# Two-layer cross attention in float32: layer 0's softmax weights are normalised in place and split by ScalarE and GpSimd, and the order of the work is written anew

## The chip, the cores and the metric

The kernel runs on one core of a Trainium2 chip. The metric is the device time of one execution, in microseconds. In the profile PE is TensorE (PEld its weight loads), DVE is VectorE, ACT is ScalarE, POOL is GpSimd, and SP only issues DMAs here. L12 is line 12 of the kernel's file.

## The reference

For each of 8 batches, x is [512, 256] and ctx is [1601, 128], all float32:

```python
# layer 0: softmax over axis 1, which is the 512 rows of x, for each of the 1601 columns
q = x @ Wq0 + bq0; k = ctx @ Wk0 + bk0; v = ctx @ Wv0 + bv0
w = softmax(q @ k.T * 256**-0.5, axis=rows_of_x)
x = layernorm(w @ v + x, eps=1e-6) * gamma + beta
# layer 1: softmax over the 1601 keys
Q = x @ Wq1 + bq1; K = ctx @ Wk1 + bk1; V = ctx @ Wv1 + bv1
out = x + (softmax(Q @ K.T * 256**-0.5, axis=keys) @ V) @ Wo + bo
```

## The kernel before, in words

The projections are folded: with A = Wq Wk^T the scores are (x A + b) ctx^T, so neither k nor v is ever made, and the weights act on ctx itself (128 columns) before one product with Wv. ctx is cut into 13 tiles of 128 rows (`MT` = 13, the last has 65), x into 4 row tiles of 128 (`TB` = 4).

Almost every large product keeps float32's accuracy by `split3`: an operand is held as a high part (rounded to the `fp32r` type) and a low part (exact minus high), and three matmuls go into one PSUM bank: w_lo times m_hi, w_hi times m_lo, w_hi times m_hi (L407 to L409, whoever calls them). ScalarE makes the high parts, VectorE or GpSimd the low ones.

Layer 0 for tile i (steps are functions of one batch and a tile number):

- `scores0` (PE): scores of 128 ctx rows against all 512 rows of x, in one of two banks of `ps_l0`.
- `max0` (DVE, L839): adds the bias row, scales, and finds the extreme of each row, out to `s0_sb`.
- `exp0` (ACT, L707): the exponential into `p0`, with its row sum; `recip0` (DVE, L846): 1/sum into `r0`.
- `p0_high` (ACT, L716): p0 times r0, rounded to `p0_hi`; `p0_low` (DVE, L851): p0 times r0 minus p0_hi, into `p0_lo`.
- `weigh0` (PE): p0_hi and p0_lo against ctx_hi and ctx_lo, summed over the 13 tiles in `ps_acc0`.
- `sum_weights` (POOL, L1034, L1037, L1039): adds p0_lo and then p0_hi to `wsum`, two additions a tile (one for the first).

`p0`, `p0_hi` and `p0_lo` have 5 places each (`ring0`: tile 12 has its own, the others take turns in four). Then `sum_rows0` (PE), `bias_x0` (DVE, L873), `weighed0` (ACT) and `at0_low` (DVE, L820), `predict` (PE), `residual0` (L883), `moments0`, `rsqrt_var` (POOL, L1058), `normalised` (L904), `turn_y` (PE, L483), `y_turned` (ACT, L729), `project_q1` (PE, L489), `q1_high` (ACT, L733), `q1_low` (DVE, L918).

Layer 1 for row tile t: `scores1` makes its 1601 scores in four chunks, one to a bank (402, 402, 402, 396 columns); `rowmax1` (DVE, L926) takes the maximum of each chunk, `bias1_of` (DVE, L934, L937) joins the four and adds the row's bias; `exp1` (ACT, L746) takes three banks and then the fourth. Then for each of the 13 ctx tiles `turn_p1` (PE transposes, L513), `p1_turned` (ACT, L754), `p1_low` (DVE, L858), `weigh1` (PE); at the end `project_out` (L527), `finish` (DVE, L953), and `residual1` on POOL (L1048, L1052) for the residual.

The order of the work is written out by hand. Four tables (`TENSOR_ORDER`, `SCALAR_ORDER`, `VECTOR_ORDER`, `GPSIMD_ORDER`) hold, for one body, each engine's steps; every engine runs its own in order, and semaphores hold them together. A body works on three batches at once: "c" is the newest (its first layer-0 tiles), "a" the one whose layer 0 it ends, "b" the one whose layer 1 it does:

```python
pre[0]()
body(None, None, batch(0, 0), AHEAD)
pre[1]()
body(batch(0, 0), None, batch(0, 1))
with eng.Fori(0, PAIRS) as pair:          # PAIRS = 3
    body(batch(pair, 1), batch(pair, 0), batch(pair, 2))
    body(batch(pair, 2), batch(pair, 1), batch(pair, 3))
body(batch(PAIRS, 1), batch(PAIRS, 0), None)
body(None, batch(PAIRS, 1), None)
```

So the pipeline fills in two bodies, six full bodies follow, then one without a "c", and one with a "b" alone. A full body begins on DVE with `q1_low`, whose eight starts in the trace (96.33, 159.77, 226.33, 291.98, 357.68, 424.67, 491.70 and 546.52 us) are taken as the edges of the bodies. The loop's semaphore waits are against registers. ctx is loaded by SP into one buffer `ctx_sb`, x by ACT's queue into two.

## Time and profile before

| what | value |
|---|---|
| median of 3 runs | 582.12 us (580.67 to 584.35) |
| span of the profiled execution | 583.1 us |
| its own time | the page gives the span alone; it lies within the runs' range |
| DVE busy | 493.2 us, 85% of the span |
| PE busy | 488.3 us, 84% |
| POOL busy | 368.2 us, 63% |
| ACT busy | 334.3 us, 57% |
| DMA | 17.25 MB, 30 GB/s on average |

Shares of the whole span mix the filling and the emptying of the pipeline with its steady part; what paces a body is read from windows laid on the bodies. A matmul's end in the profile is modelled, so a matmul's cost is read from start to start. Several engines' instructions overlap their neighbours a little (an instruction's write-back runs beside the next one), so sums of durations lie above busy time. The granted TensorE clock stands as PEclk in the windows, as a share of 2.4 GHz.

### The profile page before, as it was taken

Reading aid. Unit: us, or ns where it says so; the run is one execution under the profiler, and the core shown is the slowest. Engines: PE = TensorE matmul, PEld = TensorE weight load, DVE = VectorE, ACT = ScalarE, POOL = GpSimd, SP = SyncE. Lnnn points to the kernel's source line nnn. Section 1 sums busy time; section 2 is a strip of 40 time slices with the busy share of each in tenths; the row PEclk is TensorE's granted clock in tenths of the full one; section 3 lists DMA queues with packets and bytes.
Section 4 is the critical chain, followed back from the end, with each engine's and each line's share of the span. In section 5 each row is a group of like instructions: output and inputs, shape, how many; then the busy total and the mean of one; then the engine's idle time right before and its main releaser. Section 6 shows DMA issues by size and latency. Waiting matters only on the chain.

```text
span 583.1 us, 8934 instructions
## 1 busy us (share of the span) xinstructions
PE 488.3 (84%) x2426; PEld 397.4 (68%) x2426; DVE 493.2 (85%) x1088; ACT 334.3 (57%) x694; POOL 368.2 (63%) x319
## 2 busy tenths in 40 slices
PE   8679477898789987898889987898978986799777
PEld 8466355786578865786567865686767865677665
DVE  2577689889997988889998999889997999778864
ACT  3546634685457843785566843785546834573362
POOL 0377968757595848767695848767586758753400
...
DMA packets 23900, 17.25 MB, mean 30 GB/s; under 512 B 1055, under 2 KB 23854, under 8 KB 23854
## 3 DMA queue, kind: packets, MB, share of 16 engines
...
## 4 chain that ended last, share of the span: by engine, by line
DVE 40%; PE 36%; issue 15%; POOL 4%; ACT 4%; DVEq 1%; ACTq 0%; POOLq 0%
DVE p_lo L851 6%; PE ps_s L407 6%; DVE p1T_lo L858 5%; PE ps_s L409 4%; PE ps_s L408 4%; DVE max L926 4%; PE ps_l L407 4%; PE ps_s L513 4%; PE ps_l L409 4%; PE ps_l L408 4%; DVE xr L912 3%; DVE xr L873 3%; DVE bias L937 3%; DVE s_sb L839 3%; DVE xhat L904 2%
## 5 line engine op out<-in xcount | busy, mean ns | idle before, releaser
L1037 POOL TENSOR_TENSOR wsum<-wsum,p_lo 128x512 f32<-128x512 f32 x96 | 131.7, 1372 | 107.0 <-DVE p_lo L851 103.7
L1039 POOL TENSOR_TENSOR wsum<-wsum,p_hi 128x512 f32<-128x512 f32 x96 | 128.2, 1336 | 7.5
L707 ACT ACTIVATE p<-s_sb,min 128x512 f32<-128x512 f32 (+1 forms) x104 | 75.0, 722 | 70.2 <-DVE min L839 70.2
L851 DVE SCALAR_TENSOR_TENSOR p_lo<-p,r,p_hi 128x512 fp32r<-128x512 f32 (+1 forms) x104 | 103.6, 1008 | 2.0 <-ACT p_hi L716 2.0
L839 DVE CUSTOM_DVE_ANT_0 s_sb<-ps_l,cb 128x512 f32<-128x512 f32 (+1 forms) x104 | 70.4, 682 | 17.4 <-PE ps_l L409 13.6
L716 ACT ACTIVATE p_hi<-p,r 128x512 fp32r<-128x512 f32 (+1 forms) x104 | 74.8, 726 | 15.3 <-DVE r L846 10.4
L746 ACT ACTIVATE p<-ps_s,bias 128x1206 f32<-128x1206 f32 (+1 forms) x60 | 55.3, 925 | 47.5 <-DVE bias L937 47.4
L926 DVE TENSOR_REDUCE max<-ps_s 128x1 f32<-128x402 f32 x120 | 65.3, 570 | 19.0 <-PE ps_s L409 18.7
L407 PE MATMUL ps_s<-ctxT_hi,qw_lo 128*128 128x402 f32 x120 | 47.7, 398 | 35.9 <-DVE qw_lo L918 23.0
L858 DVE TENSOR_TENSOR p1T_lo<-ps_s,p1T_hi 128x512 fp32r<-128x512 f32 (+1 forms) x104 | 68.3, 679 | 8.9 <-ACT p1T_hi L754 8.9
L754 ACT CAST p1T_hi<-ps_s 128x512 fp32r<-128x512 f32 (+1 forms) x104 | 58.5, 586 | 22.3 <-PE ps_s L513 17.9
L513 PE MATMUL ps_s<-ident,p 128*128 128x128 f32 (+1 forms) x416 | 60.4, 280 | 4.1 <-ACT p L746 4.1
L513 PEld LDWEIGHTS ps_s<-ident,p 128*128 128x128 f32 (+1 forms) x416 | 52.0, 145 | 14.8 <-ACT p L746 4.8
L407 PEld LDWEIGHTS ps_s<-ctxT_hi,qw_lo 128*128 128x128 f32 x120 | 24.6, 205 | 46.1 <-DVE qw_lo L918 26.8
L407 PE MATMUL ps_l<-p_hi,ctx_lo 128*128 128x512 f32 (+1 forms) x104 | 48.7, 468 | 3.7 <-POOL ctx_lo L1025 3.7
L407 PE MATMUL ps_s<-p1T_hi,ctx_lo 128*128 128x512 f32 (+1 forms) x104 | 46.2, 444 | 0.0
L407 PE MATMUL ps_l<-qw_hi,ctxT_lo 128*128 128x512 f32 (+1 forms) x104 | 44.1, 424 | 0.6 <-DVE min L839 0.6
L408 PE MATMUL ps_s<-ctxT_lo,qw_hi 128*128 128x402 f32 x120 | 44.4, 370 | 0.0
L409 PE MATMUL ps_s<-ctxT_hi,qw_hi 128*128 128x402 f32 x120 | 44.4, 370 | 0.0
L408 PE MATMUL ps_l<-p_lo,ctx_hi 128*128 128x512 f32 (+1 forms) x104 | 42.6, 410 | 0.0
L409 PE MATMUL ps_l<-p_hi,ctx_hi 128*128 128x512 f32 (+1 forms) x104 | 42.6, 410 | 0.0
L409 PE MATMUL ps_l<-qw_hi,ctxT_hi 128*128 128x512 f32 (+1 forms) x104 | 42.0, 404 | 0.0
...
## 6 DMA issues: line engine op xcount, KB each, us to landing
...
```

The lines of the kernel that those rows point to most:

```text
L407: nc.tensor.matmul(ps, w_lo, m_hi, start=start, stop=False)
L408: nc.tensor.matmul(ps, w_hi, m_lo, start=False, stop=False)
L409: return nc.tensor.matmul(ps, w_hi, m_hi, start=False, stop=stop)
L513: mm = nc.tensor.transpose(ps_turn[i % 3][0:m, t * P:(t + 1) * P], p1[:, t, i * P:i * P + m], ident[:])
L707: nc.scalar.activation(p0[0:m, ring0(i), :], s0_sb[0:m, (a.par + i) % 2, :], ACT.Exp, bias=min0[0:m, i:i + 1], scale=-1.0, accum_out=sum0[ ...
L716: nc.scalar.activation(p0_hi[0:m, ring0(i), :], p0[0:m, ring0(i), :], ACT.Copy, scale=r0[0:m, i:i + 1]).then_inc(p0_hi_done, 1)
L839: nc.vector.tensor_tensor_reduce(out=s0_sb[0:m, (a.par + i) % 2, :], in0=ps_s0[0:m, (a.par + i) % 2, :], in1=cb[a.par][0:m, :], scale=-SCA ...
L851: nc.vector.scalar_tensor_tensor(p0_lo[0:m, ring0(i), :], p0[0:m, ring0(i), :], r0[0:m, i:i + 1], p0_hi[0:m, ring0(i), :].bitcast(F32), AL ...
L858: nc.vector.tensor_tensor(p1T_lo[0:m, i % RING, :], ps_turn[i % 3][0:m, :], p1T_hi[0:m, i % RING, :].bitcast(F32), ALU.subtract).then_inc( ...
L926: nc.vector.tensor_reduce(max1[:, t, k:k + 1], s1_banks(b, t)[:, k, 0:min(hi, M) - lo], AX_X, ALU.max).then_inc(max1_done, 1)
L1037: nc.gpsimd.tensor_tensor(total, total, lo, ALU.add).then_inc(wsum_part, 1)
L1039: nc.gpsimd.tensor_tensor(total, total, hi, ALU.add).then_inc(wsum_done, 1)
```

## The change

- `norm0` is new (ACT): it multiplies `p0` by `r0` in place. `p0_high` becomes a plain cast of the normalised `p0` (ACT), and `p0_low` moves from DVE to POOL as one subtraction.
- `sum_weights` adds the normalised `p0` itself: one addition a tile, and tiles 0 and 1 in one instruction (12 in all instead of 25).
- `p0` keeps its 5 places; `p0_hi` and `p0_lo` have 3. `exp0` now waits until `weigh0` and `sum_weights` are done with the tile before it in its place, and `p0_high` and `p0_low` wait for `weigh0` three tiles back. `SPLIT` names the tiles that are split; it holds all 13, so the other branch of `weigh0` is not taken.
- `rowmax1` takes two banks at a time (2 x 402 columns, two instructions a row tile instead of four). For that the fourth chunk is shifted to begin at column 1199, so that it is 402 wide too; `exp1` skips what overlaps. `bias1_of` is a tensor_scalar instead of a scalar_tensor_tensor.
- `ctx_sb` has two buffers; its loads wait for the batch two before. x is loaded by SP instead of ACT's queue. Batch 1's ctx is loaded at the start.
- The loop over pairs is unrolled, so all waits are on constants.
- All four order tables are new. `project_q1` now stands last in PE's table and `q1_high` near the end of ACT's, and PE does two tiles of `scores0` and one of `weigh0` before the first `scores1`.

```diff
-    ("q1_low", "b", 0), ("max0", "a", 6), ("p0_low", "a", 5), ("rowmax1", "b", 0), ("rowmax1", "b", 1),
+    ("q1_low", "b", 0), ("max0", "a", 6), ("max0", "a", 7), ("rowmax1", "b", 0), ("rowmax1", "b", 1),
...
+    R0 = 4
+    RH = 3
+    SPLIT = tuple(range(MT))
...
+        back, last = (1, i) if i == MT - 1 else ((0, i - R0) if i >= R0 else (1, i + MT - 1 - R0))
+        return None if back and first(a) else (back, last)
...
+    def split_before(a, i):
+
+        j = SPLIT.index(i) - RH
+        if j >= 0:
+            return MT * a.n + SPLIT[j] + 1
+        return None if first(a) else MT * (a.n - 1) + SPLIT[j] + 1
+
+    def summed(n, i):
+
+        return (MT - 1) * n + max(i, 1)
...
-    chunks = [(c, min(MPAD, c + CHUNK)) for c in range(0, MPAD, CHUNK)]
+    chunks = [(c, c + CHUNK) for c in range(0, last_lo, CHUNK)] + [(M - CHUNK, M)]
+    skip = last_lo - (M - CHUNK)
...
-            with eng.Fori(0, PAIRS) as pair:
+            for pair in range(PAIRS):
...
-                if a and c:
+                if b and c:
+                    sp.wait_ge(xbias_done, c.n - 1)
+                    load_x(c)
                     for g in range(GROUPS):
                         load_ctx(c, g, after=True)
...
             def exp0(a, i):
                 act.wait_ge(s0_read, MT * a.n + i + 1)
-                if (n := before0(a, i)) is not None:
-                    act.wait_ge(p0_lo_done, n)
+                if (held := before0(a, i)) is not None:
+                    back, last = held
+                    act.wait_ge(pv0_ps, MT * (a.n - back) + last + 1)
+                    act.wait_ge(wsum_done, summed(a.n - back, last))
...
+            def norm0(a, i):
+                act.wait_ge(r0_done, MT * a.n + i + 1)
+                m = rows(i)
+                nc.scalar.activation(p0[0:m, ring0(i), :], p0[0:m, ring0(i), :], ACT.Copy, scale=r0[0:m, i:i + 1]
+                                     ).then_inc(norm0_done, 1)
+
             def p0_high(a, i):
-                act.wait_ge(r0_done, MT * a.n + i + 1)
-                if (n := before0(a, i)) is not None:
-                    act.wait_ge(pv0_ps, n)
-                    act.wait_ge(wsum_done, n)
+                act.wait_ge(norm0_done, MT * a.n + i + 1)
+                if (held := split_before(a, i)) is not None:
+                    act.wait_ge(pv0_ps, held)
                 m = rows(i)
-                nc.scalar.activation(p0_hi[0:m, ring0(i), :], p0[0:m, ring0(i), :], ACT.Copy, scale=r0[0:m, i:i + 1]
-                                     ).then_inc(p0_hi_done, 1)
+                nc.scalar.copy(p0_hi[0:m, split_place(i), :], p0[0:m, ring0(i), :]).then_inc(p0_hi_done, 1)
...
-            def p0_low(a, i):
-                dve.wait_ge(p0_hi_done, MT * a.n + i + 1)
-                m = rows(i)
-                nc.vector.scalar_tensor_tensor(p0_lo[0:m, ring0(i), :], p0[0:m, ring0(i), :], r0[0:m, i:i + 1],
-                                               p0_hi[0:m, ring0(i), :].bitcast(F32), ALU.mult, ALU.subtract
-                                               ).then_inc(p0_lo_done, 1)
...
-                nc.vector.tensor_reduce(max1[:, t, k:k + 1], s1_banks(b, t)[:, k, 0:min(hi, M) - lo], AX_X, ALU.max
+                nc.vector.tensor_reduce(max1[:, t, k:k + 1], s1_banks(b, t)[:, 2 * k:2 * k + 2, 0:CHUNK], AX_XY, ALU.max
                                         ).then_inc(max1_done, 1)
...
-                nc.vector.scalar_tensor_tensor(bias1[:, t:t + 1], neg_max1[:, t:t + 1], c1[:, t:t + 1], c1[:, t:t + 1],
-                                               ALU.subtract, ALU.add).then_inc(bias1_done, 1)
+                nc.vector.tensor_scalar(bias1[:, t:t + 1], neg_max1[:, t:t + 1], c1[:, t:t + 1], c1[:, t:t + 1],
+                                        ALU.subtract, ALU.add).then_inc(bias1_done, 1)
...
-                    pool.wait_ge(wsum_done, MT * a.n + i)
-                    nc.gpsimd.tensor_tensor(total, total, lo, ALU.add).then_inc(wsum_part, 1)
-                    pool.wait_ge(wsum_part, (MT - 1) * a.n + i)
-                    nc.gpsimd.tensor_tensor(total, total, hi, ALU.add).then_inc(wsum_done, 1)
+                    pool.wait_ge(wsum_done, summed(a.n, i - 1))
+                    nc.gpsimd.tensor_tensor(total, total, p0[0:m, ring0(i), :], ALU.add).then_inc(wsum_done, 1)
+
+            def p0_low(a, i):
+                pool.wait_ge(p0_hi_done, split_count(a.n, i))
+                if (held := split_before(a, i)) is not None:
+                    pool.wait_ge(pv0_ps, held)
+                m, h = rows(i), split_place(i)
+                nc.gpsimd.tensor_tensor(p0_lo[0:m, h, :], p0[0:m, ring0(i), :], p0_hi[0:m, h, :].bitcast(F32),
+                                        ALU.subtract).then_inc(p0_lo_done, 1)
```

What stands on the engines at three places. First DVE, where a full body begins (`qw_lo` is the low part of layer 1's query, `s_sb,min` the scores of layer 0, `max` the maxima of layer 1). Before:

```order
L918 SCALAR_TENSOR_TENSOR qw_lo<-ps_s,scaled,qw_hi 128x512
L318 ISA
L839 ISA s_sb,min<-ps_l,cb 128x512
L839 ISA min 128x1
L851 SCALAR_TENSOR_TENSOR p_lo<-p,r,p_hi 128x512
L925 ISA
L926 TENSOR_REDUCE max<-ps_s 128x1
```

The same place now:

```order
L944 SCALAR_TENSOR_TENSOR qw_lo<-ps_s,scaled,qw_hi 128x512
L872 ISA s_sb,min<-ps_l,cb 128x512
L872 ISA min 128x1
L872 ISA s_sb,min<-ps_l,cb 128x512
L872 ISA min 128x1
L951 TENSOR_REDUCE max<-ps_s 128x1 x2
L959 TENSOR_REDUCE neg_max<-max 128x1
L962 TENSOR_SCALAR bias<-neg_max,c 128x1
```

`p_lo` is gone from DVE, a second tile of layer 0's scores stands in its place, and two reductions do for four.

Second PE, at the turn from one body to the next: the last product of a body is `project_q1` (`xhT,a_gamma`), and the first product of layer 1's scores reads `qw_lo`. Before:

```order
L489 MATMUL ps_s<-xhT,a_gamma 128x512 x2
L407 MATMUL ps_l<-p_hi,ctx_lo 128x512
L408 MATMUL ps_l<-p_lo,ctx_hi 128x512
L409 MATMUL ps_l<-p_hi,ctx_hi 128x512
L407 MATMUL ps_s<-ctxT_hi,qw_lo 128x402
```

And now:

```order
L520 MATMUL ps_s<-xhT,a_gamma 128x512 x2
L432 MATMUL ps_l<-p_hi,ctx_lo 128x512
L433 MATMUL ps_l<-p_lo,ctx_hi 128x512
L434 MATMUL ps_l<-p_hi,ctx_hi 128x512
L432 MATMUL ps_l<-qw_hi,ctxT_lo 128x512
L433 MATMUL ps_l<-qw_lo,ctxT_hi 128x512
L434 MATMUL ps_l<-qw_hi,ctxT_hi 128x512
L432 MATMUL ps_l<-qw_hi,ctxT_lo 128x512
L433 MATMUL ps_l<-qw_lo,ctxT_hi 128x512
L434 MATMUL ps_l<-qw_hi,ctxT_hi 128x512
L432 MATMUL ps_s<-ctxT_hi,qw_lo 128x402
```

Two tiles of `scores0` (six matmuls) have come in between `project_q1` and the first product that needs its result.

Third POOL, around `residual1` (the eight instructions on `y_res`). Before:

```order
L1037 TENSOR_TENSOR wsum<-wsum,p_lo 128x512
L1038 ISA
L1039 TENSOR_TENSOR wsum<-wsum,p_hi 128x512
L1022 ISA
L1025 TENSOR_TENSOR ctx_lo<-ctx_sb,ctx_hi 128x512
L1046 REGISTER_ALU
L1048 TENSOR_TENSOR y_res<-xhat,gamma_row 128x256 x4
L1052 TENSOR_TENSOR y_res<-y_res,betaob_row 128x256 x4
```

And now, with what stands behind it:

```order
L1079 TENSOR_TENSOR y_res<-xhat,gamma_row 128x256 x4
L1083 TENSOR_TENSOR y_res<-y_res,betaob_row 128x256 x4
L1062 TENSOR_TENSOR wsum<-wsum,p 128x512
L1069 TENSOR_TENSOR p_lo<-p,p_hi 128x512
L1062 TENSOR_TENSOR wsum<-wsum,p 65x512
L1069 TENSOR_TENSOR p_lo<-p,p_hi 65x512
L1050 TENSOR_TENSOR ctx_lo<-ctx_sb,ctx_hi 128x512
L1069 TENSOR_TENSOR p_lo<-p,p_hi 128x512 x2
L1059 TENSOR_TENSOR wsum<-p 128x512
L1089 TENSOR_TENSOR rstd<-var_eps,neg_half 128x2 x2
```

`residual1` has moved from the body's start to the place between tiles 10 and 11, and PE's low parts now come from this queue.

## Rows read from the trace of the kernel before

**Rows 1.** The page: busy time (1), DVE by slice (2), chain that ended last (4).

```profile
PE 488.3 (84%) x2426; PEld 397.4 (68%) x2426; DVE 493.2 (85%) x1088; ACT 334.3 (57%) x694; POOL 368.2 (63%) x319
DVE  2577689889997988889998999889997999778864
...
DVE 40%; PE 36%; issue 15%; POOL 4%; ACT 4%; DVEq 1%; ACTq 0%; POOLq 0%
```

**Rows 2.** Busy time by window: filling, first full body, a middle one, the last but one.

```profile
core 0: us, PE busy (x) PEld busy (x) DVE busy (x) ACT busy (x) POOL busy (x), PEclk, DMA share, GB/s
45.00:96.33 51.33, 35.37 (x143) 25.62 (x140) 40.43 (x91) 26.50 (x55) 40.19 (x31) 0.83 0.07 24
96.33:159.77 63.44, 55.25 (x290) 45.07 (x290) 59.79 (x134) 40.79 (x85) 44.10 (x39) 1.00 0.08 25
291.98:357.68 65.70, 57.09 (x290) 46.26 (x290) 61.02 (x134) 40.92 (x85) 46.49 (x40) 0.97 0.08 23
491.70:546.52 54.82, 46.71 (x228) 38.02 (x228) 43.92 (x105) 27.58 (x57) 30.48 (x29) 0.94 0.03 10
```

**Rows 3.** Waits on PE, 291.98 to 357.68: total, times, longest, in us.

```profile
PE ps_s L407 <- DVE qw_lo L918: 3.1, 1, 3.1
PE ps_l L407 <- DVE at_lo L820: 2.6, 1, 2.6
PE ps_s L407 <- ACT p L746: 1.4, 2, 1.0
```

**Rows 4.** Groups by line, DVE, 291.98 to 357.68: busy us, mean ns | idle before.

```profile
L851 DVE SCALAR_TENSOR_TENSOR p_lo<-p,r,p_hi 128x512 fp32r<-128x512 f32 (+1 forms) x13 | 13.2, 1023 | 0.0
L926 DVE TENSOR_REDUCE max<-ps_s 128x1 f32<-128x402 f32 (+1 forms) x16 | 8.5, 568 | 1.3 <-PE ps_s L409 1.3
L937 DVE SCALAR_TENSOR_TENSOR bias<-neg_max,c 128x1 f32<-128x1 f32 x4 | 3.3, 824 | 0.1
```

**Rows 5.** One line's instructions: ns min/median/max over the run, L851, L858, L937, L896.

```profile
L851 DVE SCALAR_TENSOR_TENSOR p_lo<-p,r,p_hi x104: 727/745/2648, 22.5 to 525.8; 128x512 fp32r<-128x512 f32 x96, 65x512 fp32r<-65x512 f32 x8
L858 DVE TENSOR_TENSOR p1T_lo<-ps_s,p1T_hi x104: 662/679/693, 122.7 to 574.8; 128x512 fp32r<-128x512 f32 x96, 65x512 fp32r<-65x512 f32 x8
L937 DVE SCALAR_TENSOR_TENSOR bias<-neg_max,c x32: 219/392/1369, 100.5 to 558.0; 128x1 f32<-128x1 f32 x32
L896 DVE TENSOR_SCALAR var_eps<-mv x16: 169/170/352, 83.3 to 540.1; 128x2 f32<-128x2 f32 x16
```

**Rows 6.** Groups by line, ACT, 291.98 to 357.68.

```profile
L716 ACT ACTIVATE p_hi<-p,r 128x512 fp32r<-128x512 f32 (+1 forms) x13 | 9.3, 726 | 2.5 <-PE ps_l L409 2.3 <-DVE r L846 0.2
L677 ACT CAST ctx_hi<-ctx_sb 128x512 fp32r<-128x512 f32 (+1 forms) x4 | 2.0, 535 | 0.0
```

**Rows 7.** Groups by line, POOL, 291.98 to 357.68.

```profile
L1037 POOL TENSOR_TENSOR wsum<-wsum,p_lo 128x512 f32<-128x512 f32 (+1 forms) x12 | 16.2, 1353 | 13.1 <-DVE p_lo L851 12.7
L1039 POOL TENSOR_TENSOR wsum<-wsum,p_hi 128x512 f32<-128x512 f32 (+1 forms) x12 | 16.2, 1346 | 0.9
L1048 POOL TENSOR_TENSOR y_res<-xhat,gamma_row 128x256 f32<-128x256 f32 x5 | 4.2, 859 | 2.2 <-DMA out_dram<-y_res 2.2
L1052 POOL TENSOR_TENSOR y_res<-y_res,betaob_row 128x256 f32<-128x256 f32 x4 | 2.8, 738 | 0.1
```

**Rows 8.** Timeline of PE: start us, duration us, instruction; places in a middle body.

```profile
296.20 0.39 PE L407 MATMUL ps_l<-qw_hi,ctxT_lo 128*128 128x512 f32 x1
296.43 0.39 PE L408 MATMUL ps_l<-qw_lo,ctxT_hi 128*128 128x512 f32 x1
...
329.35 0.60 PE L513 MATMUL ps_s<-ident,p 128*128 128x128 f32 x4
329.70 0.47 PE L407 MATMUL ps_s<-p1T_hi,ctx_lo 128*128 128x512 f32 x1
```

**Rows 9.** Timeline of POOL while the pipeline fills.

```profile
64.19 1.29 POOL L1039 TENSOR_TENSOR wsum<-wsum,p_hi 128x512 f32<-128x512 f32 x1
65.63 2.20 POOL L1037 TENSOR_TENSOR wsum<-wsum,p_lo 128x512 f32<-128x512 f32 x1
```

111 lines of the change are left out of this document (58 added, 53 removed), and 105 rows, old and new, of tables (GPSIMD_ORDER, SCALAR_ORDER, TENSOR_ORDER, VECTOR_ORDER).

## The prediction

> **What bounds the kernel now.** I read the page's busy times first, then windows laid on the bodies, then the waits and groups inside one body. The page has DVE at 85% and PE at 84% [rows 1], which settles nothing: both shares hold the filling at the start, where DVE's digits in the first slices are 2, 5, 7. The chain that ended last is 40% DVE and 36% PE [rows 1]. The windows decide [rows 2]. Six full bodies run from 96.33 to 491.70 us, (491.70 - 96.33)/6 = 65.9 us each. In a middle one of 65.70 us DVE is busy for 61.0 (93%), PE 57.1, POOL 46.5, ACT 40.9. The reader should see that DVE hardly ever waits there: its largest group, `p_lo`, has 0.0 us idle before it and the maxima 1.3 [rows 4]. PE waits 3.1 us for `qw_lo`, 2.6 for `at_lo`, 1.4 for `exp1` [rows 3], and at the first two the one waited for is DVE. So a body's pace is DVE's queue, and PE comes close behind.
>
> **DVE, per full body.** `p0_low` goes: 13 instructions, 13.2 us [rows 4]. They take 727 ns at least but 1023 in the mean, up to 2648, while `p1T_lo`, which reads PSUM, stays within 662 to 693 [rows 5]. So about 13 x 0.28 = 3.6 of the 13.2 us are not work but something that strikes instructions with both inputs in SBUF, when POOL is at work. The Trainium skill's page "SBUF — State Buffer", section "SBUF: two separate sides", says that VectorE and GpSimd share a pair of ports as an exclusive lock, which an instruction with two SBUF inputs also takes; the trace agrees in 745 ns at the median against 2648 at most.
>
> The maxima: 16 instructions at 568 ns, 8.5 us [rows 4], become 8 over twice the columns. No row shows that; one lies between 0.57 us (all fixed cost) and 1.14 (all by columns). I take 0.97, nearer the upper, since the columns are read at one rate: 7.8 us, 0.7 saved (bounds 4.0 saved and 0.6 lost). The bias as tensor_scalar: from 3.3 us for four to between 4 x 0.17 (`var_eps`, [rows 5]) and 3.3 (it meets POOL as before); I take 2.0. DVE comes to 61.0 - 13.2 - 0.7 - 1.3 = 45.8 us.
>
> **ACT.** `norm0` has the form that `p0_high` had, 726 ns, so the old 9.3 us stay; new are 13 casts from SBUF. The casts of ctx average 535 ns with one short one among four [rows 6]; I take 0.6: 7.8 us. Bounds: 0.5 and 0.73 each, 6.5 and 9.5. ACT comes to 40.9 + 7.8 = 48.7 us. x's DMA leaves its queue; SP issues it at the start of a body, with nothing but stores and ctx loads on that queue, and x is needed some 4 us of matmuls later, so I cost it at nothing.
>
> **POOL.** 24 additions at 1353 and 1346 ns and the first tile's single one go, 32.4 us plus about 1.3 [rows 7]; 12 additions and 13 subtractions of the same shape come, 25 x 1.35 = 33.8 us. POOL stays at 46.5 us. But its work is now in front of `weigh0`, where it stood behind.
>
> **PE.** Nothing is added or removed but 6 columns in a few products. The first full body, at a granted clock of 1.00, has 55.25 us busy in 63.44; the middle one at 0.97 has 57.1 [rows 2]. So with DVE at 45.8, POOL 46.5 and ACT 48.7, PE is the bound at 55.3 us plus what it waits. Before it waited 8.2 us in the first full body and 8.6 in the middle one. What remains:
> - `qw_lo`, 3.1 before. PE now has two tiles of `scores0` in front, 6 matmuls at 0.23 start to start [rows 8] = 1.4 us, and DVE reaches `q1_low` sooner. I take 0.5 (bounds 0 and 1.7).
> - `at_lo`, 2.6 before. DVE came late to the row sums because of its queue. 0.8 (0 to 2.6).
> - `exp1`, 1.4 before: the chain maxima, bias, exponential is as long as it was, with more on ACT. 1.0 (0.5 to 2).
> - The rest, 1.1 to 1.5 before: 0.8 (0.5 to 1.5).
> - New: `p0_high` waits for `weigh0` three tiles back. Queued behind it on ACT are `exp1` and the norms, and `scores1` waits for `exp1`. 0.5 (0 to 3).
> Sum 3.6 us, a body of 58.9, 7.0 saved, 42.0 in six.
>
> **Unrolling.** The registers and branches go; no wait of the loop's edge shows in the windows, whose full bodies differ by their order alone. I cost it at nothing, between 3 us gained and 3 lost in all.
>
> **Filling.** From 45 to 96.33 us neither DVE (40.4) nor PE (35.4) is full, but POOL works through `wsum` almost without a gap, with instructions of 2.20 and others of 1.29 us [rows 9]. The count of POOL's instructions ahead of the row sum is the same; what it loses to meeting `p0_low` on DVE goes, about 0.9 in the worst pair, some 2.5 us in this stretch. I take -2.5 (bounds -4 and +3, since `weigh0` now waits for POOL here). ctx of batch 1 loads earlier, ahead of weights that only the second body uses: nothing.
>
> **The last two bodies.** The last but one, 54.82 us, has PE busy 46.7 and DVE 43.9 [rows 2]; about 10 of DVE's go, PE's waits shrink: -3 (0 to -6). The last (583.1 - 546.52 = 36.6 us) has no layer 0: -0.5 (-1 to 0).
>
> **Sum.** 583.1 - 42.0 - 2.5 - 3 - 0.5 = 535.1 us. The span is 1.0 us above the median of the runs and within their spread, so I leave it: **535 us**.
>
> **Rivals.**
> *GpSimd's latency holds the body (B).* For: PE cannot start `weigh0` until ACT has normalised and cast and POOL has subtracted, 0.73 + 0.6 + 1.35 = 2.7 us where it was 0.73 + 0.74 = 1.5. Between tiles 10 and 11 POOL has `residual1`, four and four at 0.86 and 0.74 [rows 7] = 6.4 us, then an addition and the subtraction, 9.1 in all; PE has there six groups of transposes at 0.35 and five `weigh1` at 0.70 [rows 8], 5.6 us. If POOL comes to tile 10 without a lead, PE stands 3.5 us. Against: POOL has 12 us of slack a body and three places ahead. It would give 58.9 + 3.5 = 62.4 a body, so 6 x 3.5 = 21.0 saved, and 583.1 - 21.0 - 3 = 559 us.
> *The pace was a chain, not DVE's load (D).* For: 36% of the chain is PE, 15% issue. Against: DVE at 93% in the body. Then only POOL's meetings with DVE are won, about 5 us: 578 us, within 1%.
> *Slower (C).* The ring of three: `p0_high` stands in ACT's queue until PE is through with a tile that itself waits for POOL, and `exp1` behind it holds `scores1`. Each of the 13 tiles whose POOL instruction is laid bare costs 1.35 us; from (65.9 - 58.9)/1.35 = 5.2 tiles a body it eats the gain. With 8 tiles: 58.9 + 10.8 = 69.7, 3.8 a body more than before, 583.1 + 22.8 = 606 us. Against it: the order puts several steps between the three for most tiles.
> The Trainium skill's "GPSIMD Engine Reference", section "Elementwise — side-by-side cycle accounting", speaks against the change: elementwise work with two inputs is to stay on VectorE, GpSimd being about twice as slow. The trace agrees in the ratio, 1.35 to 0.745 us. By that rule alone the slower case (C, 0.07) should win; I think it does not decide, since POOL's own total is unchanged.
>
> **How the numbers follow.** Forecast 0.66, B 0.21, D 0.06, C 0.07. Low end: every wait on PE but 1.0 us goes, 56.3 a body, 57.6 saved, with -4, -6 and -1: 514.5. High end: PE's waits stay at 8.2 us, 63.5 a body, 14.4 saved, filling +3: 572. The range is 516 to 562; above it lie D, C and the end of B. A difference of over 1% is about what a measurement of this kernel can tell from none: faster 0.87 (forecast and B), same 0.06 (D), slower 0.07 (C).
>
> **What would show it.** Right: full bodies of 57 to 61 us; DVE near 46 of them, ACT near 49, POOL 45 to 47, PE over 90% at a clock of 0.97 to 1.00; its wait on `qw_lo` under 1.7. `bias` and `xhat` would still have some long instructions. Wrong: PE idle before the products with `p_hi` put down to `p_lo` on POOL in many tiles (B, C); `exp1` late with its bias long ready (C); bodies still of 65 us with DVE at 46 (D). A body above 62.4 us would make the forecast wrong, and PE busy far from 55 would make its main term wrong.

## The result, and the profile after

The changed kernel takes 516.96 us (median of four runs, 513.53 to 518.86) where the kernel before takes 581.39 in the same session: a ratio of 0.886, 95% interval 0.881 to 0.891. Forecast was 535 us, range 516 to 562. The direction was right, and so was the cause of the largest part (`p0_low` leaves VectorE, e2 below); the gain was 64 us and not 47. The profiled execution took 513.5 us, its span is 511.7. It is the shortest of the four, 3.4 us below the median, so its bodies may be some 0.6 us shorter than usual (3.4 over six, an estimate).

The page of the changed kernel: busy times, the chain that ended last.

```profile
PE 464.3 (91%) x2426; PEld 381.0 (74%) x2426; DVE 387.2 (76%) x920; ACT 385.2 (75%) x798; POOL 346.2 (68%) x319
...
PE 41%; DVE 36%; ACT 8%; issue 8%; DMA 4%; POOL 2%; SPq 0%; DVEq 0%; POOLq 0%; ACTq 0%
```

Against [rows 1] DVE fell from 493.2 to 387.2 us and PE from 488.3 to 464.3 with the same 2426 instructions. "issue" (time in which an engine waited for nothing that the profile shows) fell from 15% to 8%, and there is a new member, DMA with 4%. Both are looked at below, and neither share is a price: unrolling alone brings "issue" from 15% to 9% in the kernel before and wins nothing (e10), and taking x's load off the path wins nothing that can be told from noise (e5).

Windows of the changed kernel, laid as in [rows 2]: filling, first full body, a middle one, the last but one, the last.

```profile
core 0: us, PE busy (x) PEld busy (x) DVE busy (x) ACT busy (x) POOL busy (x), PEclk, DMA share, GB/s
45.00:85.84 40.84, 33.78 (x137) 23.24 (x135) 27.53 (x72) 29.41 (x62) 32.07 (x27) 0.87 0.11 34
85.84:141.63 55.79, 54.24 (x290) 45.20 (x290) 47.22 (x112) 47.07 (x98) 43.31 (x39) 1.00 0.02 6
255.06:311.95 56.89, 54.38 (x290) 45.16 (x290) 47.50 (x114) 47.15 (x98) 43.22 (x39) 1.00 0.12 34
425.21:474.17 48.96, 42.56 (x225) 34.68 (x225) 35.66 (x89) 33.62 (x68) 31.36 (x30) 1.00 0.04 14
474.17:511.70 37.53, 28.02 (x147) 24.22 (x147) 20.76 (x36) 15.73 (x30) 5.62 (x8) 0.95 0.06 19
```

The bodies begin, as in the prediction, where DVE starts `q1_low` (L944). Six full bodies run from 85.84 to 425.21, 56.6 us each where they were 65.9. PE is busy 54.4 of 56.9 us, at a granted clock of 1.00 (2.4 GHz). By stage, the forecast's changes against the measured ones:

| stage | forecast | measured |
|---|---|---|
| six full bodies | -42.0 | -56.0 |
| filling, up to the first edge | -2.5 | -10.5 |
| last but one body | -3 | -5.9 |
| last | -0.5 | +0.9 |

What PE waits for in the middle body, to be held against [rows 3]:

```profile
PE ps_s L432 <- DVE qw_lo L944: 1.3, 1, 1.3
PE ps_l L448 <- DMA x_sb<-in_x_dram: 0.9, 1, 0.9
PE ps_l L432 <- DVE min L872: 0.2, 1, 0.2
```

The waits on `at_lo` and on `exp1` are gone, in the first full body as in this one. The load of `x`, which the forecast had costed at nothing, is there. Groups by line in the same body: DVE (against [rows 4, 5]), ACT (against [rows 6]), POOL (against [rows 7]).

```profile
L951 DVE TENSOR_REDUCE max<-ps_s 128x1 f32<-128x804 f32 x8 | 7.9, 993 | 1.4 <-PE ps_s L434 1.2
L938 DVE CUSTOM_DVE_ANT_0 xr<-xhat,u_gamma,c_const 128x256 f32<-128x256 f32 x4 | 4.7, 1236 | 0.1
L899 DVE SCALAR_TENSOR_TENSOR xr<-bv_row,rowsum,x_sb 128x256 f32<-128x256 f32 x4 | 2.7, 727 | 0.1
L962 DVE TENSOR_SCALAR bias<-neg_max,c 128x1 f32<-128x1 f32 x4 | 1.1, 272 | 0.1
...
L750 ACT CAST p_hi<-p 128x512 fp32r<-128x512 f32 (+1 forms) x13 | 7.9, 618 | 0.1
...
L1069 POOL TENSOR_TENSOR p_lo<-p,p_hi 128x512 fp32r<-128x512 f32 (+1 forms) x13 | 16.9, 1309 | 12.0 <-ACT p_hi L750 12.0
L1062 POOL TENSOR_TENSOR wsum<-wsum,p 128x512 f32<-128x512 f32 (+1 forms) x11 | 14.4, 1305 | 0.4
```

POOL is idle 12 us ahead of `p0_low`, so it waits for ACT, and PE does not wait for it. On DVE a few instructions with both inputs in SBUF are still struck, that is, lengthened while GpSimd works: `bias_row1` (L938) most, 1236 ns in the mean where one takes 480 at its shortest, and `bias_x0` (L899), 727 ns where the kernel e9 below has 479. How that looks at the turn of a body, DVE's timeline of the changed kernel (start, duration, instruction):

```profile
302.83 1.38 DVE L930 TENSOR_SCALAR xhat<-xr,mv,rstd 128x256 f32<-128x256 f32 x4
304.36 0.48 DVE L938 CUSTOM_DVE_ANT_0 xr<-xhat,u_gamma,c_const 128x256 f32<-128x256 f32 x1
304.77 0.08 DVE L938 DVE_READ_ACCUMULATOR2_ANT c<- 128x1 f32 x1
304.77 1.50 DVE L938 CUSTOM_DVE_ANT_0 xr<-xhat,u_gamma,c_const 128x256 f32<-128x256 f32 x1
306.20 0.08 DVE L938 DVE_READ_ACCUMULATOR2_ANT c<- 128x1 f32 x1
306.20 1.49 DVE L938 CUSTOM_DVE_ANT_0 xr<-xhat,u_gamma,c_const 128x256 f32<-128x256 f32 x1
...
309.02 0.86 DVE L978 SCALAR_TENSOR_TENSOR y_res<-ps_s,r,y_res 128x256 f32<-128x256 f32 x2
309.81 0.67 DVE L872 CUSTOM_DVE_ANT_0 s_sb<-ps_l,cb 128x512 f32<-128x512 f32 x1
...
311.95 0.75 DVE L944 SCALAR_TENSOR_TENSOR qw_lo<-ps_s,scaled,qw_hi 128x512 fp32r<-128x512 f32 x1
```

The first takes 0.48 us, each of the next three 1.5. POOL's timeline shows what stands beside them; the first begins before POOL does, the others run beside its instructions:

```profile
304.63 2.77 POOL L1069 TENSOR_TENSOR p_lo<-p,p_hi 128x512 fp32r<-128x512 f32 x2 [1.63 <-ACT p_hi L750]
307.35 2.89 POOL L1062 TENSOR_TENSOR wsum<-wsum,p 128x512 f32<-128x512 f32 x2
```

All four stand ahead of the last step before the stores (`finish`), of `max0` of tile c5, and of `q1_low`. SP issues the two stores when `finish` is done, and x's load behind them:

```profile
309.92 1.78 SPq L420 DMA_DIRECT2D out_dram<-y_res  x2
311.74 0.47 SPq L366 DMA_DIRECT2D x_sb<-in_x_dram  x1
```

It lands some 4.2 us after it is issued (the median of this kernel's eight loads of x). So the prediction's "PE is the bound" was close, and yet the edge of a body was set by a queue on DVE.

### The profile page after: what moved, and what is told of

Read it like the earlier page. It is cut to its first block, busy times and chain, and to the rows that moved or that the text cites. A ratio compares the mean times of both kernels' runs of the same rounds, so it can differ in the third digit from the quotient of the medians.

```text
span 511.7 us, 7981 instructions
## 1 busy us (share of the span) xinstructions
PE 464.3 (91%) x2426; PEld 381.0 (74%) x2426; DVE 387.2 (76%) x920; ACT 385.2 (75%) x798; POOL 346.2 (68%) x319
## 4 chain that ended last, share of the span: by engine, by line
PE 41%; DVE 36%; ACT 8%; issue 8%; DMA 4%; POOL 2%; SPq 0%; DVEq 0%; POOLq 0%; ACTq 0%
DVE p1T_lo L884 7%; PE ps_s L432 5%; DVE xr L938 5%; PE ps_l L432 5%; PE ps_l L433 5%; PE ps_s L434 5%; PE ps_l L434 5%; PE ps_s L433 5%; DMA x_sb<-in_x_dram 4%; DVE xr L899 4%; PE ps_s L546 4%; DVE s_sb L872 3%; DVE max L951 3%; DVE y_res L978 2%; DVE xhat L930 2%
## 5 line engine op out<-in xcount | busy, mean ns | idle before, releaser
L1069 POOL TENSOR_TENSOR p_lo<-p,p_hi 128x512 fp32r<-128x512 f32 (+1 forms) x104 | 135.2, 1307 | 83.4 <-ACT p_hi L750 83.4
L1062 POOL TENSOR_TENSOR wsum<-wsum,p 128x512 f32<-128x512 f32 (+1 forms) x88 | 115.0, 1307 | 4.6 <-ACT p L742 1.3
L742 ACT ACTIVATE p<-p,r 128x512 f32<-128x512 f32 (+1 forms) x104 | 73.1, 719 | 4.4 <-DVE r L879 3.9
L951 DVE TENSOR_REDUCE max<-ps_s 128x1 f32<-128x804 f32 x60 | 59.1, 994 | 15.7 <-PE ps_s L434 13.3
L750 ACT CAST p_hi<-p 128x512 fp32r<-128x512 f32 (+1 forms) x104 | 63.4, 618 | 1.3 <-PE ps_l L434 0.7
L432 PE MATMUL ps_s<-ctxT_hi,qw_lo 128*128 128x402 f32 x120 | 43.7, 365 | 14.9 <-DVE qw_lo L944 10.9
L1050 POOL TENSOR_TENSOR ctx_lo<-ctx_sb,ctx_hi 128x512 fp32r<-128x512 f32 (+1 forms) x32 | 34.8, 1088 | 20.7 <-ACT ctx_hi L711 20.7
L432 PE MATMUL ps_l<-p_hi,ctx_lo 128*128 128x512 f32 (+1 forms) x104 | 46.5, 447 | 1.6 <-POOL p_lo L1069 1.3
L433 PE MATMUL ps_l<-qw_lo,ctxT_hi 128*128 128x512 f32 (+1 forms) x104 | 41.4, 398 | 0.0
L434 PE MATMUL ps_s<-ctxT_hi,qw_hi 128*128 128x402 f32 x120 | 41.4, 345 | 0.0
L433 PE MATMUL ps_s<-ctxT_lo,qw_hi 128*128 128x402 f32 x120 | 41.3, 344 | 0.0
```

The lines of the kernel that those rows point to most:

```text
L432: nc.tensor.matmul(ps, w_lo, m_hi, start=start, stop=False)
L433: nc.tensor.matmul(ps, w_hi, m_lo, start=False, stop=False)
L434: return nc.tensor.matmul(ps, w_hi, m_hi, start=False, stop=stop)
L742: nc.scalar.activation(p0[0:m, ring0(i), :], p0[0:m, ring0(i), :], ACT.Copy, scale=r0[0:m, i:i + 1]).then_inc(norm0_done, 1)
L750: nc.scalar.copy(p0_hi[0:m, split_place(i), :], p0[0:m, ring0(i), :]).then_inc(p0_hi_done, 1)
L951: nc.vector.tensor_reduce(max1[:, t, k:k + 1], s1_banks(b, t)[:, 2 * k:2 * k + 2, 0:CHUNK], AX_XY, ALU.max).then_inc(max1_done, 1)
```

## The experiments

Sixteen kernels ran. Each ratio is against the kernel before, run beside it on the same chip; a comparison with the changed kernel, which ran in another session, is best made by the two ratios (0.886 for the changed kernel). e13 is one profiled execution and has no ratio. Not tried alone are the new order tables, the second `ctx` buffer and the smaller rings, so what they are worth stays open.

**The change's parts on VectorE.** e1 is the kernel before with the two-bank maxima and the `tensor_scalar` bias, e7 the changed kernel without them. The cut from the code shows e7's line as the minus line.

```
+ nc.vector.tensor_reduce(max1[:, t, k:k+1], s1_banks(b, t)[:, 2*k:2*k+2, 0:CHUNK], AX_XY, ALU.max)
- nc.vector.tensor_reduce(max1[:, t, k:k+1], s1_banks(b, t)[:, k, 0:CHUNK], AX_X, ALU.max)
```

> One part of the change alone, on the kernel before: maxima over two banks (8 instructions a body for 16) and the bias as tensor_scalar. Theory (VectorE's queue paces a body of the kernel before): it takes 16 x 0.568 - 8 x 0.993 = 1.1 us and some 4 x 0.4 = 1.6 us off VectorE in each body, and nearly all of it shows: bodies of about 63.4 us for 65.9, some 565 us in all. Rival (the pace is a chain through several engines, and the gain of the whole change came from its order): under 0.5 us a body, 579 to 582 us.

e1: 575.92 us, ratio 0.992 (0.989 to 0.995). DVE's busy time in a body fell by 2.5 us (the mean of six, 60.6 to 58.1), the body by 0.8 (65.07). The theory, that nearly all of it shows and the time is 565 us, fell; the result lies nearer the rival. DVE's idle time in a body grew from 5.3 to 7.0 us. So DVE's queue did not pace everywhere in a body: ahead of `exp1`, where these instructions stand, most of what is taken from it comes back as idle time.

> The changed kernel with the layer-1 maxima taken bank by bank again (16 instructions a body in place of 8) and the bias with scalar_tensor_tensor. On VectorE that is about 2.7 us more in a body by what e1_maxima_alone showed (before against it 61 to 58.3 busy). Theory (VectorE, at 47.5 of 56.6 us, has slack, and only its instructions ahead of exp1 are on the path): 0 to 1 us a body, 517 to 523 us. Rival (the two-bank maxima are what shortens the chain from scores1 to exp1, so all of it shows): 2 to 2.7 us a body, 530 to 535 us.

e7: 521.93 us, 0.900 (0.896 to 0.905); bodies of 57.6, 1.1 more than the changed kernel. The maxima and the bias are worth some 4.5 us in the kernel before and 5 (by the medians) to 8 (by the ratios) in the changed one.

e2 is the changed kernel with `p0_low` on VectorE again, 13 steps put into its order by hand.

```
- nc.gpsimd.tensor_tensor(p0_lo[0:m, h, :], p0[...], p0_hi[...], ALU.subtract)
+ nc.vector.tensor_tensor(p0_lo[0:m, h, :], p0[...], p0_hi[...], ALU.subtract)
```

> The changed kernel with one part undone: p0_low is VectorE's again (one subtraction of two SBUF operands, 13 a body), each put into VectorE's order soon after its high part is cast. GpSimd keeps one addition a tile and has 17 us less to do. Theory (relief of VectorE made the gain): VectorE goes from 47.5 us a body to 47.5 + 13 x 0.7 to 0.9 = 57 to 59 busy and is the bound again: bodies of 60 to 63 us, 535 to 555 us in all. Rival (order, buffers and the halved additions made it): bodies stay at 57 us, under 522 us.

e2: 554.88 us, 0.953 (0.944 to 0.962). Bodies of 62.3 with DVE busy 55.0 and a clock of 0.95 to 0.97; first edge at 90.56. So this one step carries 5.8 of the 9.3 us per body and 4.7 of the 10.5 of the filling. That is an upper bound as far as the order by hand was not the best: PE waits 2.2 us for `p0_low` and 2.4 for `normalised` in a body there.

**Does TensorE pace?** The first product of each `weigh0` is left out (`ctx_lo` by `p0_hi`), 3 us of PE in a body, in the changed kernel (e3) and in the one before (e4).

```
- nc.tensor.matmul(ps, w_lo, m_hi, start=start, stop=False)
```

> The changed kernel without the first of weigh0's three products (ctx_lo times p0_hi is left out, so 13 matmuls a body fewer). Theory (TensorE paces a body now): 13 x 0.23 = 3.0 us a body off, bodies of about 53.8 us, some 22 us less over eight batches: about 496 us. Rival (a chain through ScalarE and GpSimd paces it, TensorE's business is only high): under 1 us a body, above 508 us.

> The same product left out of the kernel before. Theory (VectorE paced it): 0 to 0.7 us a body of the 3.0 show, 576 to 582 us. Rival (TensorE already shared the pace before): over 1.5 us a body, under 572 us.

e3: 514.68 us, 0.886 (0.880 to 0.893), bodies of 56.1. e4: 585.09, 1.007 (1.003 to 1.011), bodies of 66.0. Before, PE's load was worth nothing; e4 is even slower by 0.3 to 1.1%, with granted clocks of 0.92 to 0.97 in its bodies. After, some 3.0 us less of it (13 products at 0.23) gave 0.5 a body and nothing in the ratio: the theory that TensorE alone paces fell. Two of e3's six bodies ran at a clock of 0.97, the others at 1.00.

**x's load.** e5 issues it ahead of the stores:

```
- if b and c: sp.wait_ge(xbias_done, c.n - 1); load_x(c)
+ if a and c and not last(c): sp.wait_ge(xbias_done, a.n + 1); load_x(Batch(c.n + 1, a.use + 1, a.par))
```

> The changed kernel with one edit on SP: the load of x for batch c+1 is issued in the middle of the body, after bias_x0 of batch a, ahead of b's two stores, where it stood behind them at the start of the next body. Theory (a new chain, which the prediction costed at nothing: finish, store, x's load of 4.2 us, turn_x): PE's wait on x_sb, 3.4 us in five bodies, goes, and with it what is queued behind turn_x; bodies of 55.7 to 56.1 instead of 56.6, time 511 to 514 us where the changed kernel has 517. Rival (another wait, on qw_lo or on the maxima, ends at the same time): the wait on x_sb goes, others grow by as much, 516 to 518 us.

> As e5_x_early, and the first of the three products of each weigh0 is left out (ctx_lo by p0_hi; this part of the sum is missing from the output), as in e3_two_products_after, which gave 514.7. It says whether TensorE paces once x's load is off the path. Theory that TensorE's load paces with the x chain as the second limit: 3 us of PE less in a body now show for the most part, bodies of 53.5 to 54, time 497 to 503 us. Rival (the turn of the body, from the last residual through normalised, turn_y and q1_low to the first maxima, holds the body whatever PE's load is): no more than 0.7 us a body below e5, 507 to 511 us.

e5: 513.28 us, 0.884 (0.880 to 0.888). PE's wait on `x_sb` is gone and four bodies take 55.9 us, but the first two take 57.3 at a clock of 0.97; the interval overlaps that of the changed kernel, so a gain is not shown. e6, with the product left out as well: 512.14 us, 0.883 (0.879 to 0.888), bodies of 55.9. Both waits that remain at the turn are behind DVE (`qw_lo` 1.3, `min` 0.8), and e6's bodies fall in two kinds, 55.2 us at a clock of 1.00 and 56.7 at 0.97. Work taken from PE comes back as waiting, and in some bodies as a lower clock after the wait.

**The loop.** e8 is the changed kernel in the hardware loop again. SP waits only for `weigh0`, which covers its other wait, and PE's first `scores1` waits for `ctxT_low` instead of `finish`; both come ahead of the `q1_low` that it also waits for.

```
- for pair in range(PAIRS):
+ with eng.Fori(0, PAIRS) as pair:
```

> The changed kernel with the hardware loop over pairs of bodies back in place of the unrolled program (PE's wait ahead of scores1 is on ctxT_lo of the same place instead of on the stores, SP's on ctx_lo, which the one on weigh0 covers, is gone). Theory (unrolling is worth nothing, as the prediction has it): 514 to 520 us. Rival (registers, branches and register waits cost PE and the short instructions their start): 0.5 to 2 us a body, 521 to 530 us, with issue as a larger share of the chain that ended last.

e8: 531.20 us, 0.915 (0.910 to 0.920), 14 us more than the changed kernel by the medians and 17 by the ratios. Its first edge is at 86.17, so the filling is the same, but bodies take 59.6 us instead of 56.6. (The two profiled executions are further apart than the medians, 20 us, 18 of them in the six bodies.) Two windows of e8, columns as above, then DVE and ACT at the inner turn of the loop that begins the first of them:

```profile
206.41:266.27 59.86, 56.84 (x290) 47.56 (x290) 48.70 (x112) 45.21 (x94) 42.42 (x39) 0.94 0.08 23
266.27:326.28 60.01, 55.80 (x290) 46.61 (x290) 47.68 (x114) 49.14 (x102) 44.00 (x40) 0.97 0.13 38
```

```profile
203.37 0.21 DVE L880 RECIPROCAL r<-sum 128x1 f32<-128x1 f32 x2
206.41 0.75 DVE L945 SCALAR_TENSOR_TENSOR qw_lo<-ps_s,scaled,qw_hi 128x512 fp32r<-128x512 f32 x1 [2.83 <-issue]
...
205.30 0.29 ACT L712 CAST ctx_hi<-ctx_sb 65x128 fp32r<-65x128 f32 x1
208.48 0.62 ACT L751 CAST p_hi<-p 128x512 fp32r<-128x512 f32 x1 [2.88 <-issue]
```

At the turn both engines stand 2.8 us with nothing the profile could name. PE waits 4.2 us for `qw_lo` there, and what it does next runs at half the clock. PE's timeline of e8 behind that wait, and of the changed kernel behind its own:

```profile
207.31 0.67 PE L431 MATMUL ps_s<-ctxT_hi,qw_lo 128*128 128x402 f32 x1 [4.21 <-DVE qw_lo L945]
207.78 0.54 PE L432 MATMUL ps_s<-ctxT_lo,qw_hi 128*128 128x402 f32 x1
208.12 0.54 PE L433 MATMUL ps_s<-ctxT_hi,qw_hi 128*128 128x402 f32 x1
```

```profile
255.96 0.42 PE L432 MATMUL ps_s<-ctxT_hi,qw_lo 128*128 128x402 f32 x1 [1.34 <-DVE qw_lo L944]
256.22 0.35 PE L433 MATMUL ps_s<-ctxT_lo,qw_hi 128*128 128x402 f32 x1
256.40 0.34 PE L434 MATMUL ps_s<-ctxT_hi,qw_hi 128*128 128x402 f32 x1
```

Start to start is 0.34 us in e8, where the window from 207.3 to 211.4 us has a granted clock of 0.50 (1.2 GHz), and 0.18 in the changed kernel, at 1.00 (2.4 GHz) from 255.9 to 258.5. In e8's six bodies PE is busy 56.3 us in the mean for the work that takes 54.4 here: of the 3.0 us a body, some 1.9 is the clock and 1.1 waiting. The clock is lower in all six bodies (0.94 to 0.97), in those that begin at a turn of the loop and in those that don't, though in the latter PE waits only 1.3 us for `qw_lo`.

Is it the unrolling as such? e10 unrolls the kernel before and changes nothing else.

> The kernel before with one edit: the hardware loop over pairs of bodies is unrolled, the orders are its own. e8_loop_after showed that the loop put back costs the changed kernel 14 us: at the two inner turns of the loop VectorE and ScalarE stand 2.8 and 2.9 us with nothing to wait for, and TensorE's clock then is 1.2 GHz at the start of the body. In before VectorE's queue shows no such gap at 226.33 us, the same turn. Theory (the loop's edge costs only where an engine stands at the end of its queue waiting when the branch comes; in before VectorE is never done with its queue there): 576 to 581 us, no more than 1% below before. Rival (the loop costs every order the same 2 to 3 us a body, so unrolling was 14 us of the gain wherever it is done): 563 to 568 us.

e10: 582.83 us, 1.004 (1.000 to 1.007). Nothing. The loop costs one kernel 14 to 17 us and the other none. e13 looks at the reason: the loop of e8, with `bias_row1` last in DVE's order, so that there is work without a late wait in front of the branch.

> The changed kernel with the loop back, as in e8_loop_after, and VectorE's order ending in the four bias_row1, which wait for nothing that is late, as the order of before nearly does; the reciprocals of c4 and c5, which wait for ScalarE, come ahead of them. It is one look at the inner turn of the loop, not at the time. Theory (the loop's branch costs 2.8 us from the last instruction that had to wait, and is hidden by work queued behind that): at the two inner turns VectorE's gap of 2.8 us put down to issue is gone or under 0.3 us, ScalarE's of 2.9 stays. Rival (the gap is a cost of the branch itself on each engine, and before hides it in some other way): VectorE stands 2.8 us at both turns again.

e13 (527.14 us, one execution): DVE's gaps at the two inner turns are 0.91 and 0.99 us where e8 has 2.83 and 2.40; ACT's are 3.4 and 3.3 where e8 has 2.9 and 3.1. The theory holds in its direction and not in its number: there are 4.1 us of work behind the last wait, and by the theory the gap should have vanished. In the kernel before, the stretch before the branch at 226.33 us is `bias_row1` and `ctxT_low`, 4.0 us without any gap. What decides how much is hidden stays open. A row that bears on it is in DMA's part of e8: one packet of the instruction queue falls between 203.5 and 206.5 us, beside the loads of ctx and x.

```profile
q1 hardware_dynamic: 585, 0.58, 61.8%
q14 instruction: 1, 0.01, 1.6%
```

The columns are packets, MB and the share of the 16 engines' time. The Trainium skill's "Runtime: NRT & Kernel Launch", section "Instruction fetch mechanics", says that a taken branch to code outside the fetched pages has to wait for a DMA fetch. One packet in the gap is in line with that and doesn't show that the engines stood for it: in the kernel before, three packets of the same queue fall between 220 and 226.4 us, and VectorE has no gap there. That work queued behind the last wait covers the turn, whatever the turn consists of, is what e13's 0.9 us and e10 speak for.

**GpSimd.** e9 is the kernel before with one addition a tile to the row sum instead of two (the low parts of tiles 1 to 12 are missing from it).

```
- nc.gpsimd.tensor_tensor(total, total, lo, ALU.add).then_inc(wsum_part, 1)
- pool.wait_ge(wsum_part, (MT - 1) * a.n + i)
```

> The kernel before with GpSimd adding one part per tile to the row sums (the low parts of tiles 1 to 12 are left out of the sum), 13 instructions a batch instead of 25, on the same order. GpSimd has 16 us less a body. It sizes what GpSimd's work costs VectorE where both are at it, and what it costs the filling. Theory (VectorE paces before, so its struck instructions count; the additions are the half of GpSimd's work that falls beside p0_low): VectorE's busy time in a full body falls from 61 to 58 to 59, bodies of 63 to 64, the first body's edge at 90 to 93 instead of 96.33 since the row sum comes sooner; 562 to 572 us. Rival (VectorE's instructions meet other work of GpSimd as often, and the filling is held by something else): 576 to 581 us.

e9: 539.23 us, 0.927 (0.921 to 0.932), a gain of 41 us where the theory gave 8 to 18. Not one instruction of DVE was removed. A window of e9 (columns as above) and groups on DVE in that window:

```profile
207.55:268.02 60.47, 56.96 (x290) 46.55 (x290) 55.17 (x134) 40.70 (x85) 29.10 (x27) 0.97 0.12 37
```

```profile
L851 DVE SCALAR_TENSOR_TENSOR p_lo<-p,r,p_hi 128x512 fp32r<-128x512 f32 (+1 forms) x13 | 10.8, 840 | 0.0
L912 DVE CUSTOM_DVE_ANT_0 xr<-xhat,u_gamma,c_const 128x256 f32<-128x256 f32 x4 | 2.3, 633 | 0.0
L873 DVE SCALAR_TENSOR_TENSOR xr<-bv_row,rowsum,x_sb 128x256 f32<-128x256 f32 x4 | 1.7, 479 | 0.1
L937 DVE SCALAR_TENSOR_TENSOR bias<-neg_max,c 128x1 f32<-128x1 f32 x4 | 1.1, 269 | 0.1
```

In the kernel before the same four lines have these rows, in the middle body of [rows 4]:

```profile
L912 DVE CUSTOM_DVE_ANT_0 xr<-xhat,u_gamma,c_const 128x256 f32<-128x256 f32 x4 | 3.4, 914 | 0.0
L873 DVE SCALAR_TENSOR_TENSOR xr<-bv_row,rowsum,x_sb 128x256 f32<-128x256 f32 x4 | 3.4, 918 | 0.1
```

and `p_lo` 13.2, `bias` 3.3 [rows 4]. The four lines come to 23.3 us before and 15.9 in e9, and DVE's busy time to 61.0 and 55.2 (60.6 and 55.1 in the mean of six bodies): about 5.5 of the 61 us were GpSimd. The bodies are 60.7 us, 5.2 shorter, with as much idle time on DVE as before (5.6 us against 5.3), so here the whole of what DVE lost showed. The first edge is at 87.68, 8.65 earlier, with no change there but GpSimd's twelve additions. Why the filling is so much shorter stands among PE's waits of the kernel before, from 45 to 96.33 us:

```profile
PE ps_l L465 <- POOL wsum L1039: 7.4, 1, 7.4
```

PE stands 7.4 us for layer 0's row sum, which POOL ends at 72.5 us. In e9 POOL has it at 64.2 us and PE does not wait for it; in the changed kernel it is done at 64.7 and PE waits 0.3 us.

e16 is its counterpart in the changed kernel: eleven additions a batch are cut to one column (the row sums lack tiles 2 to 12).

> The changed kernel with eleven of GpSimd's twelve row-sum additions per batch cut to one column (the row sums lack tiles 2 to 12 in the output), so GpSimd has some 14 us less a body. It is to the changed kernel what e9_one_addition_before is to before (there: bodies 5.2 us shorter, first edge 8.7 us earlier). Theory (VectorE no longer paces, and is struck only where bias_row1 and few others meet GpSimd, 3 us a body, of which the turn of the body holds 2.8): bodies 1 to 2 us shorter, filling 2 to 4 us shorter, 500 to 508 us. Rival B of the prediction (GpSimd's latency holds weigh0): bodies 3 us shorter or more, under 498 us. Neither: 515 us.

e16: 507.03 us, 0.874 (0.869 to 0.878); bodies of 55.9, 0.7 less, first edge at 83.26, 2.6 earlier. PE still waits 0.9 us for x and 0.8 for `qw_lo` there. The theory had 1 to 2 us a body; GpSimd's additions are worth 0.7 in the changed kernel where they were worth 5.2 before.

**The turn of the body.** If the queue on DVE ahead of `q1_low` sets the edge, moving `bias_row1` must show it. e12 moves all four behind the maxima of tiles 6 and 7 of the next body, e11 loads x early as well.

```
- ("normalised","a",1), ("bias_row1","a",0), ("finish","b",0),
+ ("q1_low","b",0), ("max0","a",6), ("max0","a",7), ("bias_row1","b",0), ("rowmax1","b",0),
```

> The changed kernel with bias_row1 of a batch (four instructions, of which three take 1.4 us instead of 0.5 since GpSimd works beside them) moved on VectorE from ahead of finish to the next body, behind q1_low and the maxima of tiles 6 and 7. Theory (at the turn of the body VectorE's queue holds bias_row1 ahead of the maximum of tile c5, exp0, q1_high and q1_low, on which PE stands 1.3 us, and ahead of finish, behind which x is loaded): both waits go, 1.5 to 2.5 us a body, 502 to 508 us. Rival (the four instructions then stand ahead of the first maxima of layer 1, and exp1 and scores1 behind it become late by as much): 514 to 520 us.

> As e12_row1_after_q1, and x loaded early as in e5_x_early. Theory (the two are the same wait seen at two places, since finish and with it x's load come earlier anyway): within 2 us of e12_row1_after_q1, 501 to 508 us. Rival (x's load stays behind the stores and still ends last): 4 to 6 us below e12_row1_after_q1.

e12: 542.11 us, 0.933 (0.929 to 0.938); e11: 542.03, 0.934 (0.929 to 0.939). Both are some 25 us slower than the changed kernel, where the theory gave 502 to 508 us and even the rival no more than 520. PE does go through the turn without a wait, and then (e12):

```profile
274.13 1.11 PE L435 MATMUL ps_l<-ident,x_sb 128*128 128x128 f32 x4 [3.94 <-DVE xT_lo L835]
```

The four instructions, 5.5 us with their collisions, now hold the first maxima, `exp1` and `xT_low`. The theory was right on the place and wrong on DVE's slack behind it. e14 cuts the step into its four instructions: two stay, the third and fourth go between the biases of layer 1, each ahead of the bias that needs it (every bias waits for its own row only). e15 loads x early too.

```
+ ("normalised","a",1), ("bias_row1","a",0), ("bias_row1","a",1), ("finish","b",0),
+ ("bias1_of","b",1), ("bias_row1","b",2),   ...   ("bias1_of","b",2), ("bias_row1","b",3),
```

> The changed kernel with bias_row1 cut into its four instructions: two stay ahead of finish, the third goes behind the second bias of layer 1 in the next body and the fourth behind the third, each ahead of the bias that needs it. In e12_row1_after_q1 all four stood ahead of the first maxima: PE's wait on q1_low was gone, but xT_low came 3.9 us late. Theory (the turn is a chain through VectorE's queue, and it ends earlier by the two instructions of 1.4 us, while later in the body VectorE has slack): PE's waits on q1_low and x go, its clock stays at 2.4 GHz, bodies of 54.5 to 55.5, 500 to 508 us. Rival (the instructions are missed wherever they go, since the body is a chain through VectorE all along): 515 us or more.

> e14_row1_spread and x loaded early as in e5_x_early. Theory (finish comes 2.8 us earlier, and the stores with it, so most of the wait on x is gone in e14 already): 0 to 3 us below e14_row1_spread, 499 to 507 us. Rival: nothing, since the first bodies pay it back at the lower clock as in e5.

e14: **499.27 us, 0.861 (0.858 to 0.865)**; e15: 499.10, 0.861 (0.858 to 0.865). It leaves nothing out and beats both kernels; against the changed kernel's 0.886 it is some 2.8% faster. A window of e14 (columns as above) and what PE waits for between 140 and 420 us:

```profile
192.60:246.66 54.06, 53.88 (x292) 45.24 (x291) 46.73 (x113) 47.07 (x99) 43.16 (x40) 1.00 0.12 36
```

```profile
PE ps_s L419 <- ACT p L766: 0.6, 3, 0.3
```

PE is busy 53.9 of 54.1 us: by the trace TensorE is the bound here, as it was not in the changed kernel. No run takes load from PE in e14, so that is read and not tested. Between e14 and e15 no difference is shown: once `finish` comes earlier, the early x adds nothing.

## Why the prediction was right or wrong

Two terms of the sum failed, and they are nearly the whole miss. The forecast's span was 535.1 us and the measured one is 511.7, 23.4 less: 14.0 in the six bodies, 8.0 in the filling, 2.9 in the last but one, and 1.4 back in the last. The first is the unrolling, put at nothing, the second the filling, put at 2.5 us; both stand below with what they measured.

- **What bounds before: DVE.** Right in the main: e4 takes PE's load away for nothing, e9 shortens DVE's instructions and bodies follow. It did not hold everywhere in a body: e1 takes 2.5 us off DVE and the body gives 0.8. And I read DVE's 61.0 us as work, with 3.6 us of it struck in `p0_low`. e9 removes no DVE instruction and takes 5.5 us off in the mean.
- **DVE after, 45.8.** Measured 47.5. Maxima 7.9 against 7.8. The bias 1.1 against 2.0: it is not struck. What was missed is `bias_row1`, 4.7 us here with three of four at 1.5, where it was 3.4 before.
- **ACT after, 48.7.** Measured 47.2; the cast takes 618 ns, forecast 0.6, 7.9 us in all. The busy time rose by less, 6.2 us, since neighbours overlap: a sum of durations was put onto a busy time.
- **POOL after, 46.5.** Measured 43.2. The additions and subtractions take 1.31 instead of 1.35 us, 1.1 us in all; 1.3 us are `y_res` (750 ns instead of 859, and four in the window instead of five), 0.6 `ctx_lo` (1072 ns instead of 1233). That they meet fewer struck instructions on DVE fits this and is not tested.
- **PE 55.3 busy and 3.6 waiting, 58.9 a body.** Measured 54.4 and 2.2 in the mean of the six bodies, 56.6. In the middle body `qw_lo` is 1.3 against 0.5, inside its bounds; `at_lo`, `exp1` and the ring's wait are nothing against 2.3 together, `at_lo` and the ring at the low end of their bounds and `exp1` below its 0.5; x's load is 0.9, which I had costed at nothing. The sentence on x was wrong: there is something on SP's queue, the stores, and behind them DVE's `finish`. e5 shows no measurable time for it, though, since other waits stand beside it.
- **Unrolling at nothing.** This is the step that failed for the bodies. e8 shows 14 to 17 us for it, far outside the bounds of 3 that I gave. With the loop the body is 59.6 us (forecast 58.9) and the whole 531.2 (forecast 535). That the whole comes so close is in part luck: e8's six bodies are 4 us longer than forecast and its filling some 8 us shorter. The reading, no wait at the loop's edge before, was correct for that kernel, and e10 bears it out. The fault was to carry it over. By e13, which brings DVE's gap from 2.8 to 0.9 us with ready work ahead of the branch, what hid the branch before was most likely DVE's full queue at the turn, and that is what the change takes away. I asked of other costs what happens when the cover goes, and not of this one.
- **Filling -2.5.** Measured -10.5, beyond the bound of -4. I counted POOL's instructions ahead of the row sum (the same number) and one struck pair, and did not look at PE's waits there. PE stood 7.4 us for the row sum; in the changed kernel it stands 0.3. e9 shows 8.65 us from one addition a tile less, e2 4.7 from where `p0_low` is done, e16 that 2.6 more were to be had from the additions. Before, each tile's row sum needed DVE's subtraction and then two additions on POOL, one behind the other, 3.4 us a tile between 46.4 and 69.9 us; now it needs one addition of a `p0` that ACT has normalised, and with the subtractions in the same queue POOL still has the sum at 64.7 us instead of 72.5. A count of one engine's instructions does not show that.
- **Last bodies.** -5.9 against -3, within its bounds; +0.9 against -0.5, 0.9 beyond its bound of 0.
- **Rivals.** B (GpSimd's latency) is out: POOL waits 12 us a body for ACT, PE has no wait on `p0_low` in the middle body, and e16, with eleven additions a batch cut short, gains 0.7 us a body and not 3. C is out, and with it the rule to keep two-input elementwise work on VectorE does not decide here: one instruction takes 1.31 us on GpSimd, and still e2, with it on VectorE, is 38 us slower. D is out at 56.6 us a body, though e1 shows some of what it said. What was not foreseen at all is that the turn of a body, 9 us in DVE's queue from `normalised` to `q1_low`, holds the pace when no engine's load does.

The low end of the sum, every wait gone but 1.0 us and a filling of -4, is 514.5 us; the range that I gave began at 516, and its top was 562 where the sum gave 572. With the filling's measured -10.5 the same bodies would have led to 508.
